# Decoder layer on one core: decays and causal mask in one 128-row product, row scatters issued one by one, attention with the projection ahead of the head sums

## What is computed

```python
# 1: attention, 8 heads of 64, a bias by distance, softmax, output projection
x = layernorm(x + attn(x))
# 2: gated linear attention (mLSTM) of x against a context, 4 heads of 32
pcs = cumsum(log_sigmoid(fg))                       # decays
log_D = where(s >= t, pcs[s] - pcs[t], -inf) + ig[t]  # causal
m = max_t(log_D)
C = (q @ k.T / sqrt(32)) * exp(log_D - m)
h = C @ v / max(|sum_t C|, exp(-m))
x = layernorm(x + layernorm_per_head(h) * (1 + w))
# 3: mixture of experts: one shared, eight routed, the two best by the router
shared = gelu(x @ up) @ down
p = softmax(x @ router); two largest
x = layernorm(x + shared + sum_k p_k * expert_k(x))
```

## Time and profile before

| | us |
|---|---|
| median of 3 runs | 537.6 |
| the profiled execution | 536.77 |
| its span, first to last instruction | 534.8 |
| PE busy | 497.1 (93%) |
| DVE, ACT, POOL busy | 313.6, 274.6, 178.2 |
| mean granted clock of PE, share of full | 0.924 |

### The profile page before, as it was taken

How to read it: one execution, slowest core, us unless ns; L and a number is a source line. 1 busy time by engine, 2 the same in 40 slices (tenths; PEclk the granted TensorE clock), 3 DMA queues, 4 the chain that set the end, 5 groups by cost and what they waited for, 6 DMA issues and landing times.

```text
span 534.8 us, 15308 instructions
## 1 busy us (share of the span) xinstructions
PE 497.1 (93%) x5212; PEld 396.7 (74%) x5213; DVE 313.6 (59%) x1002; ACT 274.6 (51%) x623; POOL 178.2 (33%) x194
## 2 busy tenths in 40 slices
PE   8899999999889999999999679699999999999984
PEld 6577777777765566665469469599999999999731
DVE  5478777877884578857638134245444445445236
ACT  5576766676677888666418074023232233233226
POOL 5511101110000110153454745533554555555400
PEclk9899999999989999775659859889999999999999
DMA  4399500000000251111011201231222222222086
GB/s 129 101 224 205 151 2 2 2 1 4 22 3 21 62 177 42 40 56 41 27 59 41 74 26 35 67 75 37 71 66 65 64 69 68 64 66 70 36 268 204
DMA packets 47878, 37.97 MB, mean 71 GB/s; under 512 B 5456, under 2 KB 41184, under 8 KB 47824
## 3 DMA queue, kind: packets, MB, share of 16 engines
q1 hardware_dynamic: 43072, 28.10, 20.7%
q0 software_dynamic: 4320, 8.92, 4.7%
q10 hardware_dynamic: 432, 0.20, 0.1%
HBM read 19.30 MB, written 16.34 MB: 67 GB/s over the span
## 4 chain that ended last, share of the span: by engine, by line
PE 78%; DVE 8%; issue 6%; DMA 3%; ACT 2%; POOL 2%; SPq 0%; DVEq 0%; POOLq 0%; ACTq 0%
PE bank L1199 12%; PE bank L1189 12%; PE bank L1146 7%; PE bank L1032 4%; PE bank L1052 4%; PE bank L1036 4%; PE bank L834 3%; PE bank L887 3%; PE bank L836 2%; PE bank L835 2%; PE bank L877 2%; PE pair L857 2%; DMA wdn<-routed 2%; PE pair L967 2%; PE bank L979 2%
## 5 line engine op out<-in xcount | busy, mean ns | idle before, releaser
L474 POOL DMA_INDIRECT routed<-zbuf x71 | 74.3, 1046 | 79.1 <-DVE zbuf L1652 50.2
L779 ACT ACTIVATE prob<-bank 128x512 f32<-128x512 f32 x71 | 42.4, 598 | 105.2 <-PE bank L1189 103.3
L1199 PE MATMUL bank<-wdn,prob 128*128 x568 | 78.0, 280 | 0.2 <-issue 0.2
L1189 PE MATMUL bank<-cT,prob 128*128 128x128 f32 x568 | 76.3, 277 | 1.2 <-DVE cT L1639 0.5
L1189 PEld LDWEIGHTS bank<-cT,prob 128*128 128x128 f32 x568 | 68.9, 191 | 3.2 <-issue 2.3
L1199 PEld LDWEIGHTS bank<-wdn,prob 128*128 128x128 f32 x568 | 68.9, 191 | 1.2 <-issue 0.4
L1646 DVE COPY prob<-wup 128x512 f32 x71 | 30.4, 428 | 45.5 <-issue 23.3
L1146 PE MATMUL bank<-sdn,qblk 128*128 128x128 f32 x256 | 37.7, 300 | 11.2 <-issue 11.2
L459 POOL DMA_INDIRECT slots<-tkr,slot x32 | 32.1, 1002 | 40.2 <-DVE cmat L1410 14.7
L1146 PEld LDWEIGHTS bank<-sdn,qblk 128*128 128x128 f32 x256 | 34.6, 212 | 14.4 <-issue 13.9
L1652 DVE TENSOR_SCALAR zbuf<-bank,zbuf 128x128 f32<-128x128 f32 x71 | 24.9, 351 | 28.6 <-PE bank L1199 16.3
(11 more groups left out here) (284 smaller groups left out, 1035.0 us busy)
## 6 DMA issues: line engine op xcount, KB each, us to landing
slots<-x2T SPq DMA_DIRECT2D x8, 585.0 KB, 11.5
zbuf<-slots SPq DMA_DIRECT2D x71, 65.0 KB
tkr<-in_x SPq DMA_DIRECT2D x8, 256.0 KB, 3.1
cs<-in_ctx SPq DMA_DIRECT2D x8, 256.0 KB, 2.8
wup<-in_L_ffn_routed_up SPq DMA_DIRECT2D x1, 2048.0 KB, 9.4
zbuf<-tkr SPq DMA_DIRECT2D x8, 256.0 KB
wup<-routed SPq DMA_DIRECT2D x8, 256.0 KB, 3.6
wdn<-routed SPq DMA_DIRECT2D x8, 256.0 KB, 4.4
```

Source lines behind the costliest of these rows:

```text
L474: pool.indirect_dma_start(routed, bass.IndirectOffsetOnAxis(ap=xr[n][:, :].bitcast(I32)[:, DEST:DEST + 1], axis=0), yr[n % 4][:, :], None) ...
L779: act.activation(hT[:, n % 2, :], bank[2 + n % 2][:, :], ACT.Gelu).then_inc(s["hT_ok"], 1)
L1189: m = mm(bank[2 + n % 2][:, c * P:(c + 1) * P], wst[:, n % 2, c * P:(c + 1) * P], xrT[:, n % 2, :], start=True, stop=True)
L1199: m = mm(bank[6 + n % 2][:, 0:D], hT[:, n % 2, c * P:(c + 1) * P], wdn[:, bass.ds(e * (FC * D) + c * D, D)], start=(c == 0), stop=(c == FC ...
```

## The change

1. **Mask in the decay product.** `al` becomes four blocks of 128 rows. Rows that were unused hold keys (made once from the identity by POOL), and `rh` holds on these rows the running maximum of a mask scan, so the product of 128 rows gives decays and mask at once. L1038 and the `causal` and `identb` constants go. DVE writes `al` with four instructions on 8 partitions each, in place of one. POOL makes the constants in nine steps (`mask_ok`), and fewer of the earlier ones (`const_p` 20 to 16).
2. **Scatters one by one.** Each of POOL's scatters has a wait of its own, on products of PE (`dd_ps`, `u_ps`, `lg_ps`, `shu_ps`, `shk_ps`, `shd_ps`); 24 stand in groups 5 to 7, 2 at their end, 28 + 2 in the shared expert, and the last 8 in the routed loop, one after every second of the first 16 rows_out. base(6) and base(7) move behind tile 24, and DVE's loop is split there.
3. **Attention.** `values` ahead of `out_turn`, `proj` ahead of `heads`, two buffers of xT_hi and xT_lo, and x_hi(g + 2) right after x_evac(g + 2).

```diff
-N_CONST, N_TABLES = 20, 27
+IN_LOOP = 56
+N_CONST, N_TABLES, N_MASK = 16, 23, 9
...
-    al = [sb(f"al{n}", [P, P]) for n in range(2)]
+    al = [sb(f"al{n}", [P, GT, 2, S]) for n in range(2)]
...
         def x_lo(g, q):
             pool.wait_ge(s["xhi_ok"], g + 1)
-            pool.wait_ge(s["z_ps"], H * g)
+            if not isinstance(g, int) or g >= 2:
+                pool.wait_ge(s["z_ps"], H * (g - 1))
             pool.wait_ge(s["xT_ok"], g + 1)
-            pool.tensor_tensor(xT_lo[:, :], xTp[q][:, :], xT_hi[:, :], ALU.subtract)
+            pool.tensor_tensor(xT_lo[q][:, :], xTp[q][:, :], xT_hi[q][:, :], ALU.subtract)
...
+        mst = Steps(pool, s["mask_ok"])
+        key = ident[:, :].rearrange("p (i r) -> p i r", i=GT)[:, :, HR // 2:HR]
+        tiles = [P, 2 * GT, GT, HR // 2]
+        for q in range(2):
+            mst(pool.tensor_copy(al[q][:, :, :, :].rearrange("p k a (i r) -> p (k a) i r", i=GT),
+                                 key.unsqueeze(1).broadcast_to(tiles)))
+        for a in range(2):
+            mst(pool.tensor_scalar(drop_s[:, a, :].rearrange("p (i r) -> p i r", i=GT), key, BIG, None, ALU.mult))
+        mst(pool.tensor_scalar(drop_s[:, :, 0], drop_s[:, :, 0], -BIG, None, ALU.add))
...
-        def scatter(g):
+        def scatter(n):
+            t, k = n // 2, n % 2
...
+        def in_group(g):
+            first = 2 * GT * (g - 5)
+            pool.wait_ge(s["dd_ps"], GT * g + 1)
+            scatter(first)
+            pool.wait_ge(s["dd_ps"], GT * g + 2)
+            scatter(first + 1)
...
+        def in_shared(g):
+            first = 2 * GT * 3 + 2 + 4 * (g - 1)
+            pool.wait_ge(s["shu_ps"], FC * g + 2)
+            scatter(first)
+            pool.wait_ge(s["shu_ps"], FC * g + FC)
+            scatter(first + 1)
+            pool.wait_ge(s["shk_ps"], 3 * (g - 1) + 2)
+            scatter(first + 2)
+            pool.wait_ge(s["shd_ps"], g)
+            scatter(first + 3)
...
-        with pool.Fori(0, SLOT_TILES // NX) as i:
+        for t in range(2 * NX):
+            rows_out(t, t % NX)
+            if t % 2 == 0 and IN_LOOP + t // 2 < 2 * NT:
+                scatter(IN_LOOP + t // 2)
+        with pool.Fori(2, SLOT_TILES // NX) as i:
...
@@ group_a on ACT @@
-            if more:
-                x_hi(g + 1, 1 - q)
...
             if turn:
                 x_evac(g + 2, q)
+                x_hi(g + 2, q)
...
@@ group_a on PE @@
             if not first:
+                values(g)
                 out_turn(g - 1, 2)
-                values(g)
...
             if not first:
+                proj(g - 1, 2)
                 heads(g - 1, 3)
-                proj(g - 1, 2)
...
@@ qk @@
-            r = slice(k * HR, (k + 1) * HR)
             for a in range(2):
-                mm(bk[a * S:(a + 1) * S, 256:512], al[q][r, a * S:(a + 1) * S], rh[q][r, a, :, :],
-                   start=True, stop=False, skip_group_check=True)
-            mm(bk[:, 256:512], identb[:, :], causal[:, :], start=False, stop=True,
-               skip_group_check=True).then_inc(s["dd_ps"], 1)
+                m = mm(bk[a * S:(a + 1) * S, 256:512], al[q][:, k, a, :], rh[q][:, a, :, :], start=True, stop=True)
+            m.then_inc(s["dd_ps"], 1)
...
@@ front on DVE @@
-            tsc(al[g % 2][:, :], arow[:, :], a_mul[:, 0:1], a_add[:, 0:1], ALU.mult, ALU.add).then_inc(s["al_ok"], 1)
+            for k in range(GT):
+                r = slice(k * HR, k * HR + 2 * NH)
+                m = tsc(al[g % 2][r, k, :, :].rearrange("p a s -> p (a s)"), arow[r, :], a_mul[r, 0:1], a_add[r, 0:1],
+                        ALU.mult, ALU.add)
+            m.then_inc(s["al_ok"], 1)
...
-            if t in (3, 5):
-                base(NG - 2 + (t - 3) // 2)
-        with dve.Fori(1, SLOT_TILES // NX) as i:
+        with dve.Fori(1, EARLY // NX) as i:
+            for n in range(NX):
+                step(i * NX + n, n, i)
+        base(NG - 2)
+        base(NG - 1)
+        with dve.Fori(EARLY // NX, SLOT_TILES // NX) as i:
```

More of the change, by code:

```diff
@@ L107, in decoder_layer @@
     wq_lo = sb("wq_lo", [P, H, D], F32R)
-    xT_hi = sb("xT_hi", [P, W], F32R)
-    xT_lo = sb("xT_lo", [P, W], F32R)
+    xT_hi = [sb(f"xT_hi{n}", [P, W], F32R) for n in range(2)]
+    xT_lo = [sb(f"xT_lo{n}", [P, W], F32R) for n in range(2)]
     cpad = sb("cpad", [H, P])
@@ L446, in weighted @@
                                lnw[:, :].unsqueeze(1).broadcast_to([P, GT, D]), ALU.mult).then_inc(s["hlw_ok"], 1)
-        def scatter(g):
[L449 to L458, removed]
-                    pool.indirect_dma_start(slots, bass.IndirectOffsetOnAxis(ap=slot[:, k, t:t + 1], axis=0),
-                                            rows[:, t, :], None).then_inc(scat[g // 2], 16)
+        def scatter(n):
+            t, k = n // 2, n % 2
+            g = t // GT
+            if n % (2 * GT) == 0:
+                pool.wait_ge(s["slot_ok"], g // 2 + 1)
+                pool.wait_ge(s["tk_ok"], 16 * (g + 1))
+            pool.indirect_dma_start(slots, bass.IndirectOffsetOnAxis(ap=slot[:, k, t:t + 1], axis=0),
+                                    (tkr, tk1)[k][:, t, :], None).then_inc(scat[g // 2], 16)
@@ new lines, in in_group @@
+        def in_group(g):
[4 more added lines that the diff above has]
+            scatter(first + 1)
+            pool.wait_ge(s["dd_ps"], GT * g + 3)
+            scatter(first + 2)
+            pool.wait_ge(s["u_ps"], GT * g + 1)
+            scatter(first + 3)
+            pool.wait_ge(s["dd_ps"], GT * g + 4)
+            scatter(first + 4)
+            pool.wait_ge(s["u_ps"], GT * g + 2)
+            scatter(first + 5)
+            pool.wait_ge(s["lg_ps"], g - 1)
+            scatter(first + 6)
+            pool.wait_ge(s["u_ps"], GT * g + 4)
+            scatter(first + 7)
@@ L466, in _ @@
             weighted(g - 1)
-            if g >= 5:
-                scatter(g - 5)
-        for g in range(NG - 4, NG):
-            scatter(g)
+            if 5 <= g < NG:
+                in_group(g)
+        pool.wait_ge(s["x2T_ps"], NG - 1)
+        scatter(2 * GT * 3)
+        pool.wait_ge(s["lg_ps"], NG - 1)
+        scatter(2 * GT * 3 + 1)
+        for g in range(1, NG):
+            in_shared(g)
+        pool.wait_ge(s["shk_ps"], 3 * (NG - 1) + 2)
+        scatter(IN_LOOP - 2)
+        pool.wait_ge(s["shd_ps"], NG)
+        scatter(IN_LOOP - 1)
         def rows_out(t, n):
@@ L487, in x_hi @@
             act.wait_ge(s["xT_ok"], g + 1)
-            act.wait_ge(s["z_ps"], H * g)
-            act.activation(xT_hi[:, :], xTp[q][:, :], ACT.Copy).then_inc(s["xhi_ok"], 1)
+            if not isinstance(g, int) or g >= 2:
+                act.wait_ge(s["z_ps"], H * (g - 1))
+            act.activation(xT_hi[q][:, :], xTp[q][:, :], ACT.Copy).then_inc(s["xhi_ok"], 1)
         def x_evac(g, q):
@@ L633, in _ @@
         x_evac(1, 1)
+        x_hi(1, 1)
         for h in range(4, H):
@@ L828, in z_mm @@
         def z_mm(g, h):
+            xh, xl = xT_hi[g % 2], xT_lo[g % 2]
             if h == 0:
```

54 lines of the change are left out of this document (28 added, 26 removed).

## The result

The changed kernel takes 521.2 us (median; 520.0 to 524.4) beside 539.4 us for the kernel before; the ratio is 0.970, with a 95% interval of 0.963 to 0.976. Forecast were 495 us and a range of 484 to 516. The direction was right and the size was not: 42 us were expected; 14.7 came by the profiles and 18.2 by the medians. The profiled execution spans 520.1 us, 14.7 less than before.

The account below looks back on a forecast made before the run. PE was taken as the bound, by what it executes and its clock, with scatter backlogs stalling the shared expert. -5.5 - 2.5 - 13.8 - 22 + 1.5 = -42.3 took 536.77 to 494.5 us, median 495.3, forecast 495; range 484 to 516.

Parts of the forecast that it names:

- a): Attention groups: PE's waits for `o` and xT_lo go, the earlier projection costs nothing, last group +0.8; -5.5 us in sum.
- b): Second stage, groups 0 to 3: mask product goes, 128-row product costs no more, DVE's additions lie beside PE; -2.5 us.
- R4: Slower: PE idles on DVE's longer front and the clock falls in groups 0 to 3 too; 560 us, chance 0.03.
- c): Second stage, groups 4 to 7: full clock returns except one stretch in group 7, scatter stalls go; -13.8 us.
- R1: The clock does not improve, so groups 4 to 7 gain only 6.5 us; total 502.6 us, chance 0.25.
- d): Shared expert: with scatters spaced, held-up `sh_down_mm` and half of a half-clock stretch go; -22 us.
- a drain of 1.43 us each: Runs of scatters drain at 1.43 us each, POOL issues faster, and other engines get no new instructions during the backlog.
- The two held-up `sh_down_mm`: Shared expert: two of 14.24 and 11.51 us were to return to 3.95 us, saving 10.3 and 7.6.
- the half clock came with the interruption: Shared expert, router's products and twelve of the up projection, 8.57 us: undisturbed they take half, -4.3 us.
- e): Routed loop, first 16 tiles: rows_out and scatters need 34.3 us for 31.2; half of the +3.1 shows, +1.5 us.
- R3: The routed loop's scatters bring a stall of their own: loop term +9.7 us, total 503.5 us, chance 0.10.
- The cover that I counted on, four buffers: Routed loop: four rows_out buffers and the next tiles might absorb the scatters' +3.1 us, so only half was counted.

## Why the prediction was wrong

**a) Attention, forecast -5.5: about +1.7 measured** (the start, the six groups and the last group). Both waits went, as forecast. The step "a projection is one product of the size of out_turn, which is less than the cover left, so I cost it at nothing" failed: the projection, brought forward, waits itself for ACT's oT, 0.73 us in every group, so a group gained 0.58 and not 0.86; the run with the heads first shows 16.84 us for 17.18. Six times 0.58 is 3.5, of which PE's wait of 2.46 us without a releaser took most in this profile; it belongs to no step of the prediction. The first group fell from 15.98 to 14.82 us, as forecast, but began 0.8 later. And the last group, where +0.8 was put, grew by 3.6: the attention part alone lengthened it by 1.5 and the mask part alone by 2.0, with its clock down from 0.93 to 0.81 in both.

**b) Groups 0 to 3, forecast -2.5: +5.4.** The step that failed is "DVE's +0.8 us in each front lies beside PE (30.36 of 47.28 busy)". DVE had free time, but not there: the writes stand between front and the score for which PE's third `av` waits. A share of busy time was read where the order around one instruction mattered. The size was off too, 1.17 and not 0.8: I let a quarter of each write lie over the next, and four writes took 1.43 us to the next instruction, 0.36 each. The late writes brought the stage to 46.5. The rival that foresaw this, R4, had it at 0.03 and in a total far too long; it was part of the truth, one that stood beside the forecast and did not replace it.

**c) Groups 4 to 7, forecast -13.8: -12.7.** The size is right, the reason is not shown. The scatters alone gave 4.6 and the mask part alone 4.2 (66.6 for 70.8). On the other kind of chip the kernel before itself takes 56.1 us at a clock of 0.91, where the earlier trace rows have 0.68; so the narrow decay products and the mask product that c) spoke of do not by themselves hold the clock down. Stalls with the runs of scatters are the likelier reason, but spacing the scatters alone brought only 0.74, the wide product alone (with its waits) 0.84, and the whole change 0.88. Which of them does what stays open, so that the nearly right size is in part luck. R1, by which c) would give only 6.5, did not happen.

In groups 0 to 3 PE's idle time came and half clock came with it: 1.00 with 47.28 of 47.28 us busy, 0.86 with 48.64 of 52.64. In groups 4 to 7 it went the other way: 0.68 with 69.39 of 70.81 us busy, 0.88 with 51.05 of 58.07. Since a product also takes longer at half clock, busy time is part effect and part cause. The rule of the Trainium skill, TensorE: Matmul & The Clock Gate, section "What's actually happening" (the clock follows how busy PE has been), agrees with the first pair; by the profile's busy time it agrees neither with the second nor with the stretch of the earlier trace rows, which was full and fell.

**d) Shared expert, forecast -22: -18.7.** That the runs of scatters held the other engines up was right, on this kind of chip: with the scatters spaced, no idle time of ACT or DVE in the stage is put down to "remote" any more, and the scatter part alone brings the stage to 62.0. That they do it by a drain of 1.43 us each is not borne out by the packets, which kept the pace of 1.26. Some price above 1.26 may exist all the same: with five scatters in a group of 6.3 us, one each 1.26, the stage cost 3.8 us more, and DVE stood still for 9.13 us without a releaser at its end:

```profile
334.56 0.29 DVE L1700 COPY cT<-pair 128x128 f32<-128x128 f32 x1 [9.13 <-remote]
```

The two held-up `sh_down_mm` went away (all eight now take 3.7 to 3.8 us, the last two 7.31 together). The term was 3.3 us too large, and most of that is the step "the half clock came with the interruption", worth 4.3: from the router's products to the third `sh_down_mm` it is 6.96 us now (296.17 to 303.13) for 8.57, since the wait and the half clock after it stayed.

```profile
298.72 0.47 PE L1135 MATMUL pair<-wq_hi,xT_hi 128*128 128x512 f32 x1 [1.60 <-DVE wq_lo L1652]
299.92 0.63 PE L1136 MATMUL pair<-wq_hi,xT_lo 128*128 128x512 f32 x1
```

Before, PE had the same wait of 1.60 us for the same tile at that place.

**e) Loop, forecast +1.5: +10.7.** "24 x 1.43 = 34.3 us for 16 x 1.95 = 31.2" was mis-sized: it lets scatters fill time that the rows_out leave free, whereas each scatter cost the loop its full 1.3 to 1.4 us, (57.7 - 47.1)/8 = 1.3, at either spacing, and DVE stood still in the groups of three issues. R3 gave 9.7 for this term and was nearly exact; it had a chance of 0.10. The cover that I counted on, four buffers, does not help where DVE itself stops. On the other kind of chip the same eight scatters cost nothing (47.03 us), so the 10.6 us are no price of the issues as such.

The sum: b) and e) missed by 7.9 and 9.2, a) by 7.2, d) by 3.3, c) by 1.1, together 28.7; the tail of the kernel was 1.1 shorter, which leaves the 27.6 us by which -14.7 differs from -42.3.

## What to carry to other kernels

Before an added instruction is costed at nothing, look for the first instruction behind it on its engine that another engine waits for; a free share of the stage says nothing about that place. A gain that rests on relieving a backlog should be measured on more than one chip: here the kernel before loses 33 us on some chips only, 19.5 of them in the shared stage, and the same change is worth -3% or +2%. On that kind of chip scatters belong where no other indirect DMAs run, even in a denser row: moving eight out of the loop into the shared stage, and the writes of `al` behind the last score, made 0.954 of 0.970. With the first writes of `al` late too and the heads ahead of the projection again it is 0.946 on one kind of chip, an interval that overlaps the 0.954, and 0.983 on the other; of the two versions measured on both kinds it is the one that is not slower on either.

## What was not expected of the hardware

What a run of indirect DMAs does to the other engines depends on the chip: issued at a pitch of 1.26 us, a run of 16 went with 15.76 us of ACT standing still on one chip, while on another a run of 40 at the same pitch let every engine work, and the packets moved at the same pace on both. The same program took 503 and 504 us in the median on two chips, and 535 to 540 on the two others. Four DVE writes of 8 partitions x 128 columns took 1.43 us, while one of 128 x 128 takes 0.34: the cost went with their number. A product of 128 rows costs PE the same as one of 32 rows, in the changed kernel too (L1087: 0.60 us for four of 128 x 64 x 256). Why PE waited 2 to 3 us without a releaser at some 54 us in many of these runs stays open.
